# Sharing a rounding step between VectorE and GpSimd in the second 1-bit layer

## What is computed

```python
def _act_quant(x):                       # layer L2 (f2)
    scale = 127.0 / jnp.clip(jnp.max(jnp.abs(x), axis=-1, keepdims=True), 0.0001, None)
    y = jnp.clip(jnp.round(x * scale), -128, 127) / scale
    ...
def _linear_bit(x, w, g):
    xq = _act_quant(_rmsnorm(x, g))
    wq = _ternary_quant(w)
    return jnp.einsum('bsi,oi->bso', xq, wq)
swish = jax.nn.silu(_linear_bit(x, w1, g1))
x_v = _linear_bit(x, w2, g2)
h = swish * x_v
return _linear_bit(h, w3, g3)
```

## Time and profile before

| what | us |
|---|---|
| median of 3 runs (4317.56 to 4320.69) | 4318.08 |
| the profiled execution | 4321.57 |
| its span | 4319.8 |
| DVE busy (68% of the span) | 2934.5 |
| PE busy (84% of the span) | 3617.1 |
| POOL busy (37% of the span) | 1578.2 |

### The profile page before, as it was taken

The page is one execution under the profiler, slowest core; times in us unless marked ns, Lnnn a source line. Parts: engine busy times, 40 slices in busy tenths (PEclk is TensorE's granted clock), DMA queues, the critical chain, the costliest instruction groups (busy, mean ns, idle before and its releaser), DMA issues. The chain is left out here.

```text
span 4319.8 us, 46284 instructions
## 1 busy us (share of the span) xinstructions
PE 3617.1 (84%) x15168; PEld 1707.4 (40%) x15168; DVE 2934.5 (68%) x4097; ACT 1767.5 (41%) x2929; POOL 1578.2 (37%) x1094
## 2 busy tenths in 40 slices
PE   6788638999999999598999789765877777679898
PEld 2233214555555555342333444332333222234454
DVE  4888888577887773568886367354665888843663
ACT  4555322222222221344777243354655455321254
POOL 2999943111222110162000100027425999900122
PEclk7899978999999999797999899876988998989999
DMA  3455531133223211267771300010003555512420
GB/s 106 130 137 142 133 85 38 48 99 98 72 63 96 87 53 58 82 159 80 75 81 23 106 4 0 3 61 10 0 7 87 133 132 132 142 41 69 81 54 21
DMA packets 241368, 326.97 MB, mean 76 GB/s; under 512 B 40036, under 2 KB 141158, under 8 KB 240088
## 3 DMA queue, kind: packets, MB, share of 16 engines
q1 hardware_dynamic: 241160, 324.37, 31.2%
HBM read 276.33 MB, written 47.98 MB: 75 GB/s over the span
## 5 line engine op out<-in xcount | busy, mean ns | idle before, releaser
L521 POOL TENSOR_TENSOR m_dB<-m_du,m_BC 128x1024 f32<-128x1024 f32 x256 | 618.6, 2417 | 16.6 <-DVE m_du L553 16.6
L494 ACT ACTIVATE m_dA<-m_delta,m_a_neg 128x512 f32<-128x512 f32 x512 | 350.8, 690 | 484.8 <-DVE m_H_bank L588 418.2
L381 PE MATMUL m_y<-m_H,ident 128*128 128x512 f32 x512 | 294.7, 659 | 166.4 <-DVE m_H L599 166.4
L588 DVE TENSOR_TENSOR_SCAN m_H_bank<-m_dA,m_dB 128x512 f32<-128x512 f32 x256 | 315.0, 1231 | 128.5 <-POOL m_dB L521 105.7
L1631 DVE TENSOR_REDUCE a_core_minus_max<-a_core_a 128x1 f32<-128x512 f32 x512 | 317.0, 682 | 58.2 <-PE a_core_a L1457 58.2
L386 PE MATMUL m_y<-m_H,ident 128*128 128x512 f32 x512 | 291.2, 652 | 76.8 <-POOL m_H L506 76.8
L506 POOL TENSOR_TENSOR m_H<-m_H,m_BC 128x512 f32<-128x512 f32 x256 | 340.6, 1331 | 8.7 <-DVE m_H L593 7.6
L593 DVE TENSOR_TENSOR_SCAN m_H<-m_dA,m_dB 128x512 f32<-128x512 f32 x256 | 306.4, 1197 | 0.0
L1583 ACT ACTIVATE X<-a_core_s 128x512 f32<-128x512 f32 x512 | 264.7, 603 | 93.1 <-PE a_core_s L1457 93.0
L1023 POOL TENSOR_TENSOR ctxT<-ctxT,f_scales 128x1024 f32<-128x1024 f32 x48 | 104.8, 2183 | 531.7 <-DVE ctxT L848 531.7
L983 ACT ACTIVATE XN<-f_g,f_power_back 128x512 f32<-128x512 f32 x128 | 88.0, 687 | 402.3 <-PE f_g L920 402.3
(11 more groups left out here) (394 smaller groups left out, 7917.2 us busy)
## 6 DMA issues: line engine op xcount, KB each, us to landing
m_BC<-bc_rows SPq DMA_DIRECT2D x256, 512.0 KB, 4.9
XN<-in_L_ffn_w_dram SPq DMA_DIRECT2D x72, 256.0 KB, 2.7
ternary<-ctxT SPq DMA_DIRECT2D x96, 128.0 KB, 1.7
a_core_q<-a_q_parts SPq DMA_DIRECT2D x48, 256.0 KB, 12.9
a_core_k<-a_k_parts SPq DMA_DIRECT2D x48, 256.0 KB, 14.7
f_w_tern<-ternary SPq DMA_DIRECT2D x24, 512.0 KB, 6.7
f_core_q<-f_q_parts SPq DMA_DIRECT2D x24, 512.0 KB, 8.9
XN<-in_L_ffn_w_gate_dram SPq DMA_DIRECT2D x24, 256.0 KB, 2.7
```

The source lines that it names most:

```text
L381: pe.matmul(ps_y[:, 0, :], ident[:], HD[n % NH], start=False, stop=True, skip_group_check=True).then_inc(s_ad, 1)
L494: act.activation(dA[:, i % NA, :], delta[b % 2][:, e, :], ACT.Exp, scale=a_neg[:, e, k % N:k % N + 1]).then_inc(s_dA, 1)
L521: pool.tensor_tensor(dB[n % 2][:], du[b % 2][:, h * EH:(h + 1) * EH, :], BC[n % NS][:, 0:1, :].broadcast_to([P, EH, L]), ALU.mult).then_in ...
L588: dve.tensor_tensor_scan(ps_H[:], dA[:, 2 * n % NA, :], dB[n % 2][:, 0, :], 0.0, ALU.mult, ALU.add).then_inc(s_sc, 1)
```

## The change

The rings get four buffers. In f2 rows with n % 4 = 1 are rounded by GpSimd and the other three of four by VectorE; VectorE issues the rounding of row n-1 behind the product of row n. In f1 SHARE is 1, so n % 1 is never 1 and GpSimd rounds nothing there, as before; VectorE's rounding moves one row behind its product there too. Each rounding engine has its own semaphore, and TensorE and VectorE wait on the one that belongs to the row.

```diff
-    RING = 3
+    RING = 4
+    SHARE = RING if gained else 1
+
+    def pooled(n):
+        return n % SHARE == 1
+
+    def on_pool(n):
+        return sum(pooled(i) for i in range(n))
...
+        def wait_rounded(eng, n):
+            if pooled(n):
+                eng.wait_ge(s_xp, on_pool(n + 1))
+            else:
+                eng.wait_ge(s_xq, n + 1 - on_pool(n + 1))
...
             for n in range(NT * NX):
-                pe.wait_ge(s_xq, n + 1)
+                wait_rounded(pe, n)
...
-            eng.tensor_scalar(xq[n % RING][:], r1[n % RING][:], MAGIC, -MAGIC, ALU.add, ALU.add).then_inc(s_xq, 1)
+            eng.tensor_scalar(xq[n % RING][:], r1[n % RING][:], MAGIC, -MAGIC, ALU.add, ALU.add).then_inc(
+                s_xp if pooled(n) else s_xq, 1)
...
-            if gained:
-                for n in range(NT * NX):
+            for n in range(NT * NX):
+                if pooled(n):
                     rounded(pool, n)
...
                 if n >= RING:
-                    dve.wait_ge(s_xq, n - RING + 1)
+                    wait_rounded(dve, n - RING)
...
                     dve.tensor_scalar(r1[i][:], XN[:, t, :], q[:, j, t:t + 1], None, ALU.mult).then_inc(s_r, 1)
-                    rounded(dve, n)
+                if n and not pooled(n - 1):
+                    rounded(dve, n - 1)
+            rounded(dve, NT * NX - 1)
```

More of the change, by code:

```diff
@@ L2395, in quantised_input @@
         s_eps, s_rt = sem("eps"), sem("root")
-        s_c, s_r, s_xq, s_t, s_cp = sem("chain"), sem("r"), sem("xq"), sem("t"), sem("copied")
+        s_c, s_r, s_t, s_cp = sem("chain"), sem("r"), sem("t"), sem("copied")
+        s_xq, s_xp = sem("rounded_dve"), sem("rounded_pool")
         block = st.enter_context(nc.Block())
+        def wait_rounded(eng, n):
[3 more added lines that the diff above has]
+                eng.wait_ge(s_xq, n + 1 - on_pool(n + 1))
         @block.scalar
```

## The result

The changed kernel took 4289.79 us (median of 4 runs, 4288.35 to 4291.19) against 4319.39 for the kernel before (4 runs, 4317.56 to 4321.11). The ratio is 0.9931, with a 95% interval of 0.9918 to 0.9943. That is 29.6 us less, and the interval allows 25 to 35. The profiled execution took 4288.35 us with a span of 4286.6.

A forecast was written before the change was run, and what follows sets the result against it. The prediction took GpSimd's 32 roundings to pace f2's quantised_input, with VectorE the bound afterwards. Saving 28.1 us in f2 and 1.7 in f1, together 29.8, took 4318.08 to 4288.3 us, range 4283 to 4294.

The forecast's parts named there:

- What bounds the stage: f2's quantised_input: GpSimd's 32 roundings set the pace, 60.48 of 62.70 us busy; after the change VectorE becomes the bound.
- The price of a step on VectorE: VectorE's queue: by distance of starts, 0.66 us a product and 0.34 a rounding; nothing added for the new waits.
- The exclusion: f2: GpSimd's and VectorE's roundings exclude each other for the whole instruction, first comer wins; round 4.09 us, 0.45 more.
- first rival: f2: no exclusion in effect, a round of 3.64 us, 3.6 us more saved, 4284.7 us; chance 0.10.
- second rival: f2: GpSimd wins the race at 0.83, VectorE's rounding is held, round 5.63 us, 4300.6 us; chance 0.08.
- figure of 769 ns: Skill's best time for a 512-element loop on GpSimd; prediction said the row's 1.94 us does not meet it.
- Tail and sum in f2: f2: 0.66 to product 1, seven rounds 28.6, last rows 5.2; 34.5 us against 62.6, 28.1 less.
- f1: f1's rounding one row behind: a row costs 0.74 us in place of 0.86, stage 1.7 us less.
- Costs taken as nothing: Longer rings, GpSimd's waits, the third gain's load and the main block's start were each taken to cost nothing.
- The clock's first rise: f2's main block: TensorE's clock first rises at 5 us as before; if not, the slow-clock case was to hold.
- third rival: f2's main block: TensorE's clock stays low, 46 groups for a loss of 8.6 us, 4326.7 us; chance 0.01.
- The total: Whole kernel: 29.8 us less, from the median of 4318.08 to 4288.3 us; range 4283 to 4294.

The follow-up runs named there:

- e8: The kernel before with rings of four buffers in place of three, nothing else; f2 stage 62.61 us, f1 stage 15.10, total 4317.54 us (one run).
- e10: Changed kernel with GpSimd rounding one row of three up to row 28, VectorE's two roundings behind one product, rings of six; f2 stage 30.13 us, ratio 0.9918 to before.
- e11: Changed kernel with short products as fillers shifting VectorE's roundings against GpSimd's start, one group a memset, rings of ten; f2 stage 34.39 us, total 4289.21.
- e5: Changed kernel with eight groups in different orders of VectorE's products and roundings, rings of twelve; f2 stage 32.24 us, total 4278.72 (one run).
- e4: Changed kernel with one product put ahead of the VectorE rounding behind GpSimd's release, so GpSimd starts first; f2 stage 33.16 us, total 4284.73 (one run).
- e7: Changed kernel with VectorE rounding each row right behind its own product, no lag, in f1 too; f1 stage 15.10 us, f2 34.50, total 4288.70.
- e3: Changed kernel with three products behind the one that releases GpSimd, then three VectorE roundings, rings of six; f2 stage 31.92 us, ratio 0.9917 to before.
- e2: Changed kernel with rings of eight buffers, same order and one-in-four share; f2 stage 34.06 us, total 4285.75 (one run).
- e9: Changed kernel with memsets of different lengths as fillers shifting VectorE's roundings against GpSimd's start, rings of ten; f2 stage 33.12 us, total 4289.00.

## Why the prediction came out right, and what in it was wrong

- **What bounds the stage.** Right. With GpSimd's 32 roundings the stage is 62.61 us with rings of three and of four (e8); take them away and VectorE's queue sets it (32.41 of 34.10 us busy).
- **The price of a step on VectorE.** Right: 0.66 for a product and 0.34 for a rounding, read as distances of starts, hold wherever VectorE doesn't wait for its own product; e10's 2.64 for three products and two roundings is their sum to 0.02. The new waits cost nothing.
- **The exclusion.** The size was right and the mechanism too wide. Forecast were a round of 4.09, a held rounding of 0.87 and GpSimd at 2.0 to 2.1; measured 4.04, 0.82 and 2.03. But the step "the one that comes first keeps the other waiting to its end" is false for this instruction. It was read from rows in which GpSimd's instruction is a tensor_tensor. GpSimd's tensor_scalar of 512 columns has the path from about 0.15 us (1.92 less the 1.77 by which it ends behind a rounding that was there first) to about 0.6 and again for its last 0.46, estimates from e11 and e5, and between them VectorE rounds freely (e4, e5, e7). The forecast came out by luck: the two roundings of the changed order happen to fall on those stretches, and the second so near the edge that in e5's seventh group the same order ran without the hold, at the 3.64 us of the first rival. The rule of the Trainium skill named in the prediction ("SBUF — State Buffer", "Who interferes with whom") is too wide by the same: it says for the whole instruction, and the measured gap of some 0.9 us (0.6 to 1.46) decides against that for this pair of instructions. For GpSimd's tensor_tensor no run tested it.
- **The second rival** (GpSimd wins the race, 4300.6) was priced by that step and is void: with GpSimd first, the stage is 0.9 us shorter than the changed one, not 12 longer (e4).
- **The first rival** (no exclusion, a round of 3.64) didn't happen in the changed order, though e3 and the second to seventh groups of e5 run at that round. The figure of 769 ns that the prediction took from the Trainium skill ("GPSIMD Engine Reference", section 3.1) is not met by the whole instruction of 1.92 us.
- **Tail and sum in f2.** 34.5 forecast, 34.06 measured; 28.1 less forecast, 28.55 measured. Most of the difference is 7 times 0.05 in the round. (Copies back to back are 0.49 apart by the earlier trace rows, not 0.50, which changes nothing here.)
- **f1.** 1.7 forecast, 1.84 measured; e7 shows that the lag alone gives it. The row takes 0.73.
- **Costs taken as nothing.** The barrier and the start of the main block are as before (first product 0.61 behind the last copy, 0.60 before). The clock's first rise was said to stay at 5 us, and the prediction named any other value as a sign of the third rival. It came at 3.4, earlier and not later; in e8, with the stage of before, it came at 5.8 and in e7 at 3.2. The third rival, a clock that stays low, didn't occur, and the sign was set too sharply.
- **The total.** 4288.3 forecast, 4289.79 measured, inside the range: 29.6 us less against 29.8. 30.4 of the 33.2 us between the profiled spans are the two stages; the rest is scatter of other stages.

## What to carry to other kernels

When an engine with a low average load paces a stage, move its work to the engine that waits for it, and price the move by distances of starts on that queue, not by durations. Then test whether the share left behind pays: here a quarter kept on GpSimd gave nothing until VectorE's roundings were ordered around it (31.92 us with e3's order against 33.31 without the share). A pair of engines that shut each other out should be scanned by offset in one kernel, with the order varied from group to group, since one total of a 4.3 ms kernel scatters by more than all of these orders differ.

## What the runs showed of the hardware

- GpSimd's tensor_scalar on 128 x 512 (f32 to bf16, both in SBUF) takes 1.92 us. With it, VectorE's tensor_scalar of the same kind behind a product is held if it begins 0.12, 0.23 or 0.33 us behind GpSimd's start (e11), or 1.48 (e4). From 0.49 to 0.83 neither engine is touched (e4, e5, e10). At 0.17 and 0.16 ahead and at 0.03 behind, VectorE runs and GpSimd ends 1.77 or 1.78 us behind it (changed kernel, e11); at 1.16, 1.31 and 1.38 VectorE runs and GpSimd ends 0.46 us behind it (e5, e11). At 1.48 to 1.50 beside a GpSimd already stretched to 2.03 sixteen were held and one was not (changed kernel, e2, e5).
- A rounding at 0.17 right behind another one on VectorE ran unheld (e5, fifth group), and so did those at 0.08 to 0.27 behind a memset (e9).
- VectorE's products with one input in PSUM (scalar_tensor_tensor, 0.73 us) neither stretched GpSimd nor were held, at any offset tried (e3: four in a row beside 1.92 us). One memset alone didn't either (e11).
- VectorE's roundings back to back keep GpSimd out as long as they last: six of them took 2.09 us and GpSimd 3.71.
